# Relative-position attention on one core: a constant tile of the distance table left out, and the query and key rows loaded whole instead of loaded in part and copied

## The reference

```python
q, k, v = heads(h @ Wq + bq), heads(h @ Wk + bk), heads(h @ Wv + bv)
dist_idx = pos_l - pos_r + M - 1              # M = 256, l and r from 0 to 511
pos_emb = dist_emb[dist_idx]                  # the table has 2 * M - 1 = 511 rows
scores = einsum('bhqd,bhkd->bhqk', q, k)
scores = scores + einsum('bhld,lrd->bhlr', q, pos_emb) + einsum('bhrd,lrd->bhlr', k, pos_emb)
probs = softmax(scores / sqrt(D), axis=-1)
ctx = einsum('bhqk,bhkd->bhqd', probs, v)
```

## Time and profile before

| | |
|---|---|
| Time, median of 3 runs | 2888.73 us (2884.1 to 2892.21) |
| Profiled execution: own time | 2886.97 us |
| Profiled execution: span | 2885.2 us |
| Mean granted TensorE clock | 0.900 |
| PE busy (matmul) | 2521.4 us, 87% |
| DVE (VectorE) busy | 2055.5 us, 71% |
| ACT (ScalarE) busy | 1627.6 us, 56% |
| POOL (GpSimd) busy | 1883.5 us, 65% |
| distances, first to last add on VectorE | 358.3 to 1177.6 us |
| attention, first score to last | 1201.1 to 2245 us |
| HBM read, written | 417.39 MB, 352.63 MB |

### The profile page before, as it was taken

One profiled execution on the slowest core, in us unless ns is written; L12 is line 12 of the kernel. 1 busy time (PEld: TensorE's weight loads), 2 busy tenths in 40 slices (PEclk: granted clock), 3 DMA queues, 4 the chain that ended last, 5 costly groups with the idle time before them and its releaser, 6 DMA issues. The chain is left out here.

```text
span 2885.2 us, 53492 instructions
## 1 busy us (share of the span) xinstructions
PE 2521.4 (87%) x19084; PEld 1753.8 (61%) x19084; DVE 2055.5 (71%) x5771; ACT 1627.6 (56%) x2069; POOL 1883.5 (65%) x1535
## 2 busy tenths in 40 slices
PE   3988688788878888599999999999999499999998
PEld 1655477677767777366666666666666355555553
DVE  4767277667767777577777777777777388888885
ACT  1645556566556666277878778788877222222222
POOL 2333356565765564488888888888888356666664
PEclk7999777778778778599999999999999799999999
DMA  3688799999999999999999999999998312222210
GB/s 117 226 296 269 259 401 386 378 400 385 398 393 387 376 404 388 316 328 317 302 313 308 312 310 306 304 306 301 314 301 266 132 68 77 77 77 77 77 48 24
DMA packets 301960, 773.59 MB, mean 268 GB/s; under 512 B 37608, under 2 KB 104496, under 8 KB 258048
## 3 DMA queue, kind: packets, MB, share of 16 engines
q1 hardware_dynamic: 277152, 660.82, 66.6%
q10 hardware_dynamic: 17888, 86.27, 9.2%
q0 software_dynamic: 6656, 23.07, 2.3%
HBM read 417.39 MB, written 352.63 MB: 267 GB/s over the span
## 5 line engine op out<-in xcount | busy, mean ns | idle before, releaser
L952 POOL TENSOR_SCALAR t_neg<-t_neg,t_low 128x512 f32<-128x512 f32 x512 | 793.6, 1563 | 121.5 <-DVE t_low L1153 117.2
L1153 DVE CUSTOM_DVE_ANT_1 t_neg<-t_ps,t_r 128x512 f32<-128x512 f32 x1024 | 667.6, 686 | 250.5 <-issue 245.5
L1215 ACT ACTIVATE t_eT<-t_pt 128x1024 f32<-128x1024 f32 x512 | 524.3, 1024 | 211.6 <-PE t_pt L1072 211.0
L1072 PE MATMUL t_pt<-t_ident,t_neg 128*128 128x128 f32 x4096 | 617.3, 273 | 4.7 <-POOL t_neg L952 4.2
L1072 PEld LDWEIGHTS t_pt<-t_ident,t_neg 128*128 128x128 f32 x4096 | 516.4, 142 | 82.9 <-POOL t_neg L952 5.9
L1537 PE MATMUL e_pX<-e_we,e_h2T 128*128 128x512 f32 x1024 | 455.8, 596 | 14.3 <-DVE e_even L1745 14.3
L1060 PE MATMUL t_ps<-t_kb,t_qa 96*128 96x512 bf16 x1024 | 399.1, 390 | 62.0 <-DVE t_low L1153 37.2
L831 DVE TENSOR_TENSOR d_r<-d_pq,d_r 128x1024 f32<-128x1024 f32 x256 | 299.6, 1219 | 139.0 <-ACT d_r L804 103.8
L1205 ACT ACTIVATE t_neg<-t_neg,t_low 128x512 f32<-128x512 f32 x512 | 369.2, 721 | 46.3 <-DVE t_low L1153 46.3
L831 DVE TENSOR_TENSOR ad_nat<-d_pq,ad_nat 128x1024 f32<-128x1024 f32 x256 | 298.6, 1218 | 121.0 <-ACT ad_nat L804 99.5
L706 POOL COPY ad_nat<-ad_nat 32x2048 f32<-32x2048 f32 (+1 forms) x156 | 294.3, 1886 | 104.6 <-DMA ad_nat<-q_by_place_scratch 98.3
(11 more groups left out here) (156 smaller groups left out, 3269.6 us busy)
## 6 DMA issues: line engine op xcount, KB each, us to landing
t_r<-r_scratch SPq DMA_DIRECT2D x1024, 256.0 KB, 6.5
r_scratch<-d_r SPq DMA_DIRECT2D x128, 1024.0 KB, 9.3
r_scratch<-ad_nat SPq DMA_DIRECT2D x128, 1024.0 KB, 7.0
ad_nat<-q_by_place_scratch ACTq DMA_DIRECT2D x78, 256.0 KB, 6.3
q_rows_scratch<-a_part SPq DMA_DIRECT2D x16, 768.0 KB, 4.7
k_rows_scratch<-a_part SPq DMA_DIRECT2D x16, 768.0 KB, 6.7
q_by_place_scratch<-ad_nat SPq DMA_DIRECT2D x6, 2048.0 KB, 16.8
k_by_place_scratch<-ad_nat SPq DMA_DIRECT2D x6, 2048.0 KB, 19.4
```

The source lines that it names most:

```text
L952: nc.gpsimd.tensor_scalar(neg[:, j % RING, t, :], neg[:, j % RING, t, :], low[:, j % RING, t:t + 1], None, ALU.subtract).then_inc(pool_sub, 1)
L1072: last = nc.tensor.transpose(p_t[t // 2][:, t % 2, c, :], neg[:, j % RING, t, c * P:(c + 1) * P], ident[:])
L1153: nc.vector.tensor_tensor_reduce(out=neg[:, j % RING, t, :].rearrange("p (c r) -> p c r", r=TB), in0=p_s[t % 2][:].rearrange("p (c r) -> p ...
L1215: nc.scalar.activation(to, p_t[half][:], ACT.Exp, scale=(1.0 if half else -1.0)).then_inc(exped, 1)
```

## The change: what it does

- **distances** leaves the tile (rc, lc) = (0, 3) out in both groups: 30 tiles. Its constant terms are read off neighbours: `edge[:, 1]` (key term) is row 127 of the key part of tile (0, 2), one copy; `edge[:, 0]` (query term) is column 0 of tile (1, 3), copied from PSUM in 16 pieces of 8, one ahead of each add. Four VectorE instructions (`split_edge`) cut them into three bf16 parts beside rows of ones, and SyncE stores the 128 x 2 x 6 x 128 result.
- **attention** gets 6 more contraction rows (`EDGE`): three parts of the query term against ones, and ones against three parts of the key term, zero outside the tile left out. The score matmul has 102 rows instead of 96.
- The 96 rows are laid out with the part as the fastest index: each of the 6 products of parts is loaded from HBM into every sixth partition, 16 rows a load. There are no copies on VectorE and GpSimd any more. Per batch there are 24 loads of 128 KB and 4 small edge loads, issued by SyncE's queue 6 heads behind the head for which it loads `r`, two to four per head (for the first batch by ScalarE's queue, ahead of everything).
- Of `r`, the first key block (c = 0) has partitions 0 to 95 loaded (192 KB), by ScalarE's queue, one load ahead of each head's work; partitions 96 to 127 (the queries of the tile left out) are set to zero once. SyncE's queue loads the other three blocks.

The diff, cut to its core:

```diff
+        tiles = [tile for tile in tiles if tile[1:] != (0, NT - 1)]
         NTILE = len(tiles)
         new_q = [i == 0 or (tiles[i][0], tiles[i][2]) != (tiles[i - 1][0], tiles[i - 1][2]) for i in range(NTILE)]
-        new_k = [i % NT == 0 for i in range(NTILE)]
+        new_k = [i == 0 or tiles[i][:2] != tiles[i - 1][:2] for i in range(NTILE)]
...
+                for i, (g, rc, lc) in enumerate(tiles):
                     dve.wait_ge(k_out, NU * (i + 1))
                     for n in range(NU):
+                        part = r[i % 2][:, n * QL:(n + 1) * QL, :]
+                        if (rc, lc) == (0, NT - 2):
+                            if n == 0:
+
+                                later(dve, edge_done, g)
+                                nc.vector.tensor_copy(edge[:, 1, :], r[i % 2][:, TB - 1, :]).then_inc(edge_step, 1)
+                            if n == NU - 1:
+                                dve.wait_ge(edge_step, (NU + 4) * g + 1)
                         dve.wait_ge(q_units, NU * i + n + 1)
-                        part = r[i % 2][:, n * QL:(n + 1) * QL, :]
+                        if (rc, lc) == (1, NT - 1):
+
+                            nc.vector.tensor_copy(edge[:, 0, n * QL:(n + 1) * QL], pq[n % 2][:, :, 0]).then_inc(edge_step, 1)
                         nc.vector.tensor_tensor(part, pq[n % 2][:], part, ALU.add).then_inc(q_added, 1)
+                    if (rc, lc) == (1, NT - 1):
+                        split_edge(g)
...
                 for i, (g, rc, lc) in enumerate(tiles):
+                    if (rc, lc) == (1, NT - 2):
+                        sp.wait_ge(edge_done, g + 1)
+                        sp.dma_start(edge_d[g], edge_rows[:]).then_inc(edge_stored, 16)
                     for p in range(NP):
...
+        def load_rows(engine, b, half, pair, x):
+
+            tensor, parts = ((qa, A_PARTS), (kb, B_PARTS))[x]
+            first = H // 2 * half
+            at = b % 2 * H + first
+            engine.dma_start(tensor[pair:ROWS:NPAIR, 0, at:at + H // 2, :].rearrange("d h w -> d (h w)"),
+                             rows_d[x][b, parts[pair] * D:(parts[pair] + 1) * D, first:first + H // 2
+                                       ].rearrange("d h w -> d (h w)")).then_inc(batch_loaded[b % 2][half], 16)
+
+        def load_edge(engine, b, half, x):
+
+            tensor, columns = ((qa, Q_EDGE), (kb, K_EDGE))[x]
+            first = H // 2 * half
+            n = b % GB * H + first
+            at = b % 2 * H + first
+            engine.dma_start(tensor[ROWS:ROWS + EDGE, 0, at:at + H // 2, columns],
+                             edge_d[b // GB, n:n + H // 2, x].rearrange("n r l -> r n l")).then_inc(batch_loaded[b % 2][half], 16)
+
...
-                for i in range(BG):
-                    copy_k(0, i, 0)
+                for u in range(2):
+                    nc.gpsimd.memset(kb[ROWS:ROWS + EDGE, 0, u * H:(u + 1) * H, TB:S].bitcast(F32), 0.0).then_inc(k_zeroed, 1)
+                pool.wait_ge(k_zeroed, 2)
                 for n in range(NH + GH + 2):
                     head(n // U, n % U)
-                    for i, place in enumerate(K_PLACES):
-                        b = (n - place) // H + 1
-                        if (n - place) % H == 0 and 1 <= b < nb:
-                            copy_k(b, i, 2 * (n + 1))
 
...
                     later(sp, added, TT * (n - RR + 1))
-                    for c in range(NT):
+                    for c in range(1, NT):
                         src = r_d[g][c, n - g * P, 0:NT * TB * TB].rearrange("(p x) -> p x", x=TT * TB)
                         sp.dma_start(r[:, n % RR, c].rearrange("p t r -> p (t r)"), src).then_inc(r_loaded[n % RR], 16)
...
+                        done, step = divmod(H * b + j - AHEAD, H)
+                        if 0 <= done < nb - 1 and step < 2 * NPAIR:
+                            if step == 0:
+
+                                later(sp, scored, TT * H * done)
+                            for x in range(2):
+                                load_rows(sp, done + 1, step // NPAIR, step % NPAIR, x)
+                                if step % NPAIR == NPAIR - 1:
+                                    load_edge(sp, done + 1, step // NPAIR, x)
...
-                pe.wait_ge(q_copied, 2)
-                pe.wait_ge(k_copied, 1)
+                pe.wait_ge(q_zeroed, 2)
+                pe.wait_ge(k_zeroed, 2)
+                pe.wait_ge(batch_loaded[0][0], HALF)
...
                     for s in range(H // U):
                         for j in range(U):
-                            if j % GH == GH - 1 and not (last and s == H // U - 1 and j == U - 1):
-                                pe.wait_ge(q_copied, 2 * (BG * b + (U * s + j) // GH + 2))
-                                pe.wait_ge(k_copied, BG * b + (U * s + j) // GH + 2)
+                            if j == U - 1 and not (last and s == H // U - 1):
+
+                                pe.wait_ge(batch_loaded[(b + s) % 2][1 - s], HALF * ((b + s) // 2 + 1))
                             head(H // U * b + s, j)
...
-                        b, m = (n - Q_FIRST) // H + 1, (n - Q_FIRST) % H // 2
-                        if t == 1 and n % 2 == 0 and b < nb:
-                            copy_q(b, m)
...
-                for m in range((H - Q_FIRST) // 2):
-                    copy_q(0, m)
+                nc.vector.memset(r[CORNER:P, :, 0], 0.0).then_inc(r_zeroed, 1)
+                for u in range(2):
+                    nc.vector.memset(qa[ROWS:ROWS + EDGE, 0, u * H:(u + 1) * H, 0:S - TB].bitcast(F32), 0.0).then_inc(q_zeroed, 1)
+                dve.wait_ge(r_zeroed, 1)
...
+                def load_corner(n):
+
+                    later(act, added, TT * (n - RR + 1))
+                    src = r_d[n // P][0, n % P, 0:(NT - 1) * TB * TB].rearrange("(p x) -> p x", x=TT * TB)
+                    act.dma_start(r[0:CORNER, n % RR, 0].rearrange("p t r -> p (t r)"), src).then_inc(r_loaded[n % RR], 16)
+
+                def batch(b):
                     for s in range(H // U):
                         for j in range(U):
+                            n = H * b + U * s + j
+                            if n + RR - 1 < NH:
+                                load_corner(n + RR - 1)
                             head(H // U * b + s, j)
```

98 lines of the change are left out of this document (48 added, 50 removed).

## The result

The changed kernel takes 2985.66 us (median of 4 runs, 2968.83 to 2992.75) against 2888.48 of the kernel before: a ratio of 1.033, with a 95% interval of 1.028 to 1.037. The forecast was 2822 us. 97 us are lost, and 164 us lie between the forecast and the result.

A forecast was written before the change was run, and what follows sets the result against it. Distances was taken as bound by stores and fills together, attention by TensorE. -47.0 + 4 - 14.7 - 7 = -64.7 us from 2886.97 gave 2822 us, own range 2801 to 2835, stated range 2803 to 2846.

The forecast's parts named there:

- The queues in attention: Attention's loads: bytes hardly change, ScalarE's issues hide under the exponent, SyncE loads five heads ahead; cost nothing.
- Rival (3): Attention: DMA engines become the bound through the rows' loads; 2929 us if these run at 115 GB/s; chance 0.04.
- the gain by that rule: Start of attention: the skill's port rule for row loads into every sixth partition would give 10 us.
- Distances, -47.0 + 4: Distances: two tiles left out save 47.0 us; the edge's small copies ahead of adds cost 4 us.
- The interval of 23.3 us: Distances, first group: time between tile starts while nothing is loaded; expected gone, with 30.0 and 24.2 us staying.
- rival (4): Distances: the interval does not go, another tile loses the gain; 2860 us or no change; chance 0.04.
- The split, costed at nothing: Distances: the split's four VectorE instructions fall into waits ahead of a tile; 2 us per group without that cover.
- The copies in attention, -14.7: Attention: without VectorE's query copies a score comes 0.23 us sooner per group of four heads, 64 groups, -14.7 us.
- rivals (1): Attention: the tile pays, but a wait behind the removed one takes its gain, start gains nothing; 2844 us; chance 0.15.
- (2): Attention: ScalarE's chain moves with TensorE and the whole 0.46 us per group is won; 2808 us; chance 0.11.
- The start of attention, -7: Start of attention: first turn sooner without copies, against more row loads before the first score; between 1.4 and 10 us gained.
- the 4 us named as a sign: Start of attention: first turn expected within 4 us of the first score, where it was 9.1 us behind.

The follow-up runs named there:

- e5: e1 without the loads of q's and k's rows and edges for batches 2 to 15: 2843.44 us, ratio 0.9832.
- e9: e6 without the edge rows' loads from batch 2 on: 2851.34 us, ratio 0.9866.
- e6: Kernel before's attention (old row loads and copies) with changed distances, edge rows' loads and full 128-partition loads of block 0 of r: 2870.44 us, ratio 0.9915.
- e7: e1, but from batch 1 on one load of 96 adjacent partitions per half replaces six loads of 16 partitions: 2905.41 us, ratio 1.003.
- e1: Changed kernel with key block 0 of r loaded whole (128 partitions, 256 KB) by SyncE's queue: 2938.98 us, ratio 1.0175.
- e8: e6 with block 0 of r as a 96-partition load issued by SyncE: 2972.93 us, ratio 1.028.
- e14: e8 with block 0's 192 KB loaded as 128 partitions of 1.5 KB instead of 96 of 2 KB: 2850.96 us, ratio 0.987.
- e12: e8 with only the first 64 partitions of block 0 loaded (128 KB): 2929.31 us, ratio 1.0138.
- e3: Changed kernel with each group of 16 rows loaded into 16 adjacent partitions instead of every sixth: 3165.58 us, ratio 1.096.
- e10: Kernel before with one edit, block 0 of r loaded into 96 partitions on SyncE's queue: 2993.07 us, ratio 1.0359.
- e13: e6 with the left out tile's memory zero-filled during the projections and block 0 of r loaded whole from its own place: 2870.37 us, ratio 0.9939.
- e11: e8 with the 96 partitions of block 0 loaded in two loads, 64 and 32: 2980.06 us, ratio 1.0314.
- e2: Changed kernel with the same 96-partition load of key block 0, but issued by SyncE's queue: 3032.99 us, ratio 1.050.
- e4: Changed kernel with key block 0 loaded whole (128 partitions, 256 KB) by ScalarE's queue: 2940.04 us, ratio 1.0179.

## Why the prediction was wrong

The surplus, part by part, each step one pair of runs:

| step | us | total |
|---|---|---|
| forecast | | 2822 |
| no row loads from batch 2 on, full blocks (e5) | +21 | 2843.4 |
| old row loads and copies (e9) | +8 | 2851.3 |
| edge loads (e6) | +19 | 2870.4 |
| 32 more rows of q and k loaded, in wide loads, and no copies (e7) | +35 | 2905.4 |
| the same in 16 rows, every sixth partition (e1) | +34 | 2939.0 |
| corner of 96 partitions on ScalarE's queue (after) | +47 | 2985.7 |

**The step that failed** is "The queues in attention. Bytes hardly change. ... so nothing". All but the first two rows of this table belong to it, 134 us; the second is what the old row loads and copies cost. The bytes did stay (the trace reads 418.17 MB, 417.39 before). What the step didn't ask is what the DMA engines need for the same bytes in loads of another shape, and it had no margin for the answer: by the pace of 32 heads, four edge loads a batch were already more than the kernel before could bear without loss. From there on, whatever costs the engines time lengthens attention, and 0.04 was far too small a chance.

Rival (3) had the mechanism. But it priced `r` and the rest at the 390 GB/s of the distances, which left 22 us a batch for the rows' loads. At the 307 GB/s that the earlier trace rows shows for attention itself, the 16.8 MB of `r`, values and results take 55 us and the 3.15 MB of rows 10 us, together the 65 us of a batch: nothing was left. And it looked for the loss in the rows' loads alone. They cost 69 us by the table (35 and 34), but the edge loads cost 19 and the corner 47, and it priced neither. "Nothing, even at the maximum" for the issues holds for ScalarE's queue (the corner's issues took 311 ns at the median). For SyncE's queue it was said without a price, and there an issue of `r` grew from 432 to 568 ns; by e8 and e14 this goes with the shape of the loads and not with their number. The kernel before's 287.5 us of waiting there were no slack of the DMA engines, only a queue that stood five heads ahead.

The Trainium skill (SBUF — State Buffer, "Door 1: The DMA port swizzle") says that partitions 0 to 63 reach no more of the 16 ports than 0 to 31, eight, and that 0 to 127 reach all 16. I held the rule against the rows' loads and not against the corner. The runs agree with its direction: 64 partitions ran at an estimated 121 GB/s in e12, where the whole stretch with 128 ran at 307, and rows in 16 neighbouring partitions were 180 us slower than in every sixth (e3). By its table the corner puts eight partitions on half of the ports and four on the others, and the 64 partitions eight on half of them, so by this estimate both should cost what a full block costs, with eight on each; measured is more, 1.25 and 1.08 us against 0.85, and what adds the rest no run here shows. At the start of attention the gain by that rule was to be 10 us; 3.6 us came.

**Distances, -47.0 + 4:** 41.2 us were gained, 1.8 less than forecast, which is within the 5.8 us by which the end of this stage differs between executions. The interval of 23.3 us went and 30.8 and 23.9 stayed, so rival (4) was wrong. But the 4 us stood at the wrong place. The small copies take 0.15 to 0.17 us, not the 0.258 of the nearest row, and delay nothing that can be seen. The split, costed at nothing, takes 2.4 to 7.0 us in the 28 groups of the 14 executions, and in 8 of them no idle time is left behind it; in the kernel after it made tile (1, 3) 3.1 us longer.

**The copies in attention, -14.7:** the mechanism holds, the size is less. In e5, without copies, 32 heads take 129.0 us against 130.4 in the kernel before, so 0.17 us per group of four and not 0.23, about 11 us over all heads. e5 lacks the row loads too, but e14 shows that freer DMA engines alone change nothing in the 130.4 us. In the changed kernel the gain can't be seen, because TensorE isn't the bound. So rivals (1), with no gain, and (2), with 0.46 us per group, can't be judged in the changed kernel, and e5 speaks against both.

**The start of attention, -7:** from the last add to the first turn it was 32.7 us before and is 29.0 now, so -3.6 us. The first score didn't come sooner after the last add (24.4 us against 23.5), as it waits for 12 narrow loads and two of edges; the turn follows it after 4.7 us instead of 9.1, not within the 4 us named as a sign. And what the turn won was lost behind it, as e5 shows. From the last add to the score of the 33rd head it takes 164.4 us, and 157.5 in the kernel before: batch 1's row loads are still there, and from 1200 to 1250 us the DMA share is 1.04 and TensorE busy for 42.8 of 50 us.

With this the first row of the table is accounted for, profiled execution against profiled execution (2843.51 for 2886.97, 43.5 us gained of the 64.7 forecast). Distances give 1.2 us less than forecast in e5 (41.8). The first 32 heads lose 6.9 us where 8.8 were to be gained (7 and an eighth of 14.7), which makes 15.7. The other 224 heads gain 9.7 us where 12.9 were forecast, 3.2 less. What comes after the last score is 1.0 us longer. The sum is 21.1 us. The first 32 heads are thus the largest part, and the DMA share points to the DMA engines there too.

## What to carry to other kernels

A DMA share near 1 doesn't say yet that the DMA engines set the pace: it was 1.02 in e14, at TensorE's pace, and 1.03 in e10, 102 us slower. It does say that no margin can be counted on. There each load must be priced in engine time at that stage's own rate and shape, not in bytes and not at the best rate of another stage. GB/s that fall while the share stays, as here from 307 to 275, are the sign that the shape of the loads has become the cost. A load that leaves out partitions can cost more than the whole: leaving out a quarter of the block's partitions cost 0.40 us a load, leaving out a quarter of each partition saved time. If a part of a tile is not needed, cut it along the free dimension, or fill it once and load it whole, as e13 does. Untested is a layout in which the missing tile is a quarter of each partition; e14's 2851 us suggest what it could give.

## What was not expected of the hardware

- 96 partitions of 2 KB took more engine time than 128 (1.25 against 0.85 us by the estimate above); splitting them 64 and 32 didn't help (e11: 7 us more than e8).
- The corner cost 94 to 102 us on SyncE's queue with the other loads (e2, e8, e10), but 47 us on ScalarE's (the changed kernel against e1). A full block cost the same on either (e1, e4). Why a second queue halves the one surplus and changes nothing for the other stays open.
- Rows in 16 neighbouring partitions cost 180 us more than in every sixth (e3), and one load of 96 partitions 34 us less than six of every sixth (e7).
- An edge load of 12 KB in pieces of 256 bytes costs 0.34 us (e6 against e9), 40% of the estimate for a full block of 256 KB.
- A DMA share of 1.02 to 1.04 stood both beside TensorE's pace (e9, e14, the kernel before) and beside one about 10% slower (e8, e10).
- When the DMA engines are held up, SyncE's queue shows it in the length of its issues: 133 us of 200 in e14 and 183 in e8, with the same number of loads for each head.
